# GpSimd adds two rows that nobody reads after each of 128 indirect transfers, in a three-block model on one core

## Chip, core and metric

The kernel runs on one core of a Trainium2 chip. The core has five engines that work in order, each on its own instruction stream, and wait for each other by semaphores: TensorE (PE), VectorE (DVE), ScalarE (ACT), GpSimd (POOL) and SyncE (SP), which here only issues DMA transfers. The metric is the device time of one execution in microseconds (us); lower is better.

## What is computed

The input x is (8, 512, 128). The model is four residual blocks, each behind a layer norm: a delta-rule attention of 16 heads, a mixture of experts, a linear attention of 16 heads, and the same mixture of experts again.

```
x = x + delta_rule_attention(layernorm(x))
x = x + moe(layernorm(x))
x = x + linear_attention(layernorm(x))
x = x + moe(layernorm(x))

def moe(x):                       # 8 experts, 2 per token
    probs = softmax(x @ Wg)
    topw, topi = top_k(probs, 2)  # weights renormalised to a sum of 1
    h = relu(x @ W1[e])           # 128 -> 256
    y = h @ W2[e]                 # 256 -> 128
    return sum over the two experts of topw * y
```

## The kernel before

**Chunks and routes.** The sequence is cut into 8 chunks of 64 steps; a chunk holds 8 x 64 = 512 tokens, as J = 4 tiles of 128 rows. Each of the two mixtures of experts meets each chunk once. These 16 passes are called routes: 0 to 7 are the first mixture, 8 to 15 the second.

**Dense and sparse.** Routes 0 to 5 and 15 are dense: all eight experts are computed for all tokens. Routes 6 to 14 are sparse, in five groups: (6), (7, 8), (9, 10), (11, 12), (13, 14). For a sparse route GpSimd scatters the 512 normalised tokens to DRAM (`s_xs`), each to the places of its two experts: `scatter(r)`, 2 x 4 indirect transfers of 128 rows of 512 B. SP then loads a group's tokens back in tiles of 128 rows of one expert each (`tile_load`, L624, with the weights at L627), two tiles to a pair, 56 pairs in all. TensorE turns a pair (`tile_turn`, L2092), multiplies with W1 (`tile_up`, L2101) and W2 (`tile_down`, L2122); ScalarE copies between them (L1340, L1347, L1354); SP stores the result to `s_ys` (L635). When all tiles of a group are stored, GpSimd collects each token's two rows with `gather(r)`, again 8 indirect transfers, and VectorE adds them with their weights in `combine(r)` (L3118).

**Phases.** Up to about 425 us on the profile's clock the delta rule and the dense routes run, with much work on VectorE. After that TensorE works through the linear attention of 8 chunks and the 56 pairs of tiles, interleaved by hand. The dense route 15 comes last: matmuls at L1814 to L1816 and L2150, ScalarE's relu at L1175, VectorE's mixes at L2743, in eight steps. VectorE has the combines 10 to 14 between the steps of that route: combine 10 ahead of its ranking, combine 12 ahead of the first mix, combine 14 ahead of the last.

**What sets the order.** Every engine's order is written out, one line per step. No scheduler changes it. GpSimd's list after the delta phase is `lin_keep(0)`, `scatter(6)`, `lin_keep(1)`, `scatter(7)`, `scatter(8)`, `lin_keep(2)`, `lin_keep(3)`, `gather(6)`, and so on to `gather(14)`. `lin_keep(c)` (L943) is a sum of 128x512 elements that frees the buffer into which SP loads the next chunk (L536), and whose result VectorE needs in the residual (L3009). `scatter(r)` waits until VectorE has the places of the rows (`row_at`, L3043). `gather(r)` waits until the group's tiles are stored. In SP's list, `tile_load` of a group's first pair waits for all scatters of the group, and everything behind it in the list waits with it. The zero rows that pad the tiles are stored at L597.

The tile `y_odd` is used in the dense routes of the delta phase only. `bo_rows` holds a bias and is never written after its load. `bc(x, 1, J)` repeats a tile J times along a new axis, and `tt` is GpSimd's operation on two tiles.

Of the kernel before, what the change touches and what calls it, by code (L numbers as in the profile page):

```python
# [17 lines left out]

# [1 line left out]

# [6 lines left out]
ALU = mybir.AluOpType  # L29
# [11 lines left out]
J = NT // 128  # L41
# [7 lines left out]
GROUPS = ((6,), (7, 8), (9, 10), (11, 12), (13, 14))  # L49
# [24 lines left out]
def bc(ap, axis, n):  # L74

    ap = ap.unsqueeze(axis)
    shape = list(ap.shape)
    shape[axis] = n
    return ap.to_broadcast(shape)


def build(nc, d, out):
    with ExitStack() as ctx:
        def sb(name, shape, dtype=F32):
            return ctx.enter_context(nc.sbuf_tensor(name, shape, dtype))

        def sem(name):
            return ctx.enter_context(nc.semaphore(name))
# [16 lines left out]
        bo_rows = sb("bo_rows", [128, D])  # L105
# [82 lines left out]
        y_odd = sb("y_odd", [128, J, D])  # L188
# [45 lines left out]
        def slot(r):  # L234
# [16 lines left out]
                 ("pad_at", len(GROUPS) * E), ("tiles", 2 * E), ("first", MOST_TILES), ("expert", MOST_TILES),  # L251
                 ("offset", MOST_TILES), ("counts", E), ("shift", E)]
        low_at = {name: sum(size for _, size in sizes[:k]) for k, (name, _) in enumerate(sizes)}
        low = {name: oq_mem[:, low_at[name]:low_at[name] + size] for name, size in sizes}
        sel_shift = low["sel_shift"].rearrange("p (c e) -> p c e", e=E)
# [100 lines left out]
        tabled, padded, combined = sem("tabled"), sem("padded"), sem("combined")  # L356
        mid_stored, out_stored = sem("mid_stored"), sem("out_stored")
        scattered = [sem(f"scattered_{k}") for k in range(2)]
        gathered = [sem(f"gathered_{k}") for k in range(2)]
        tile_loaded = [sem(f"tile_loaded_{k}") for k in range(BUFFERS)]  # L360
        tile_stored = [sem(f"tile_stored_{k}") for k in range(len(ys))]
# [47 lines left out]
        def _(sp):  # L409
# [180 lines left out]
            def pads(g):  # L590

                sp.wait_ge(tabled, TABLE_OPS * g + 17)
                _, starts_at = nc.values_load_multi_w_load_instructions(
                    pad_at[0:1, g], engines=[mybir.EngineType.SP], min_val=0, max_val=E * ROOM[g] - TILE,
                    skip_runtime_bounds_check_because=ROWS_WHY)
                for e in range(E):
                    sp.dma_start(s_xs[g][bass.ds(starts_at[e], TILE)], zeros[:]).then_inc(padded, 16)  # L597

            def tile_load(p):

                g = sum(2 * p >= first for first in FIRST_TILE[1:])
                k = 2 * p - FIRST_TILE[g]
                sp.wait_ge(tabled, TABLE_OPS * g + 17)
                if k == 0:
                    for par in range(2):
                        mine = [r for r in GROUPS[g] if r % 2 == par]
                        if mine:
                            sp.wait_ge(scattered[par], 16 * 2 * J * (same_parity(mine[-1]) + 1))
                    sp.wait_ge(padded, 16 * E * (g + 1))
                _, at = nc.values_load_multi_w_load_instructions(  # L610
                    tile_table[0:1, g, k:k + 2, 0], engines=[mybir.EngineType.SP], min_val=0, max_val=E * ROOM[g] - TILE,
                    skip_runtime_bounds_check_because=ROWS_WHY)
                _, e = nc.values_load_multi_w_load_instructions(
                    tile_table[0:1, g, k:k + 2, 1], engines=[mybir.EngineType.SP], min_val=0, max_val=E - 1,
                    skip_runtime_bounds_check_because=EXPERT_WHY)
                if p >= BUFFERS:
                    sp.wait_ge(tile_z, p - BUFFERS + 1)
                elif p == 2:
                    sp.wait_ge(y_part, E * N1)
                elif p == 4:  # L620
                    sp.wait_ge(added, EV * N1)
                for h in range(2):
                    b = 2 * (p % BUFFERS) + h
                    sp.dma_start(xs[b], s_xs[g][bass.ds(at[h], TILE)]).then_inc(tile_loaded[p % BUFFERS], 16)  # L624
                for h in range(2):
                    b = 2 * (p % BUFFERS) + h
                    sp.dma_start(w1_tile[b], d["w1"][:, bass.ds(e[h], 1)].rearrange("p o f -> p (o f)")  # L627
                                 ).then_inc(tile_loaded[p % BUFFERS], 16)
# [159 lines left out]
        def _(pool):  # L788
# [14 lines left out]
            tt = nc.gpsimd.tensor_tensor  # L803
# [134 lines left out]
            def lin_keep(c):  # L938

                pool.wait_ge(xb_loaded, 16 * (c + 1))  # L940
                if c:
                    pool.wait_ge(x3_ready, c)
                tt(x_keep[:], x_b[:], bc(bo_rows[:], 1, J), ALU.add).then_inc(kept, 1)  # L943

            def scatter(r):

                k, g = SPARSE.index(r), GROUP_OF[r]
                pool.wait_ge(rows_ready, k + 1)
                pool.wait_ge(xf_ready, J * (r + 1))
                pool.wait_ge(o_part, NG * GROUP_OPS * NCH)  # L950
                for s in range(2):
                    for j in range(J):
                        nc.gpsimd.indirect_dma_start(  # L953
                            s_xs[g], bass.IndirectOffsetOnAxis(ap=row_at[:, k, s, j:j + 1], axis=0),
                            xf_at[r % 2][:, j], None).then_inc(scattered[r % 2], 16)

            def gather(r):

                k, g = SPARSE.index(r), GROUP_OF[r]
                last = FIRST_TILE[g + 1] // 2 - 1  # L960
                for b in range(len(ys)):
                    pool.wait_ge(tile_stored[b], 16 * len([p for p in range(last + 1) if p % len(ys) == b]))
                pool.wait_ge(tabled, TABLE_OPS * (g + 1))
                if k >= 2:
                    pool.wait_ge(combined, 2 * (k - 1))
                for s in range(2):
                    for j in range(J):
                        nc.gpsimd.indirect_dma_start(  # L968
                            gathered_at[k % 2][:, s, j], None, s_ys[g],
                            bass.IndirectOffsetOnAxis(ap=back_at[:, k, s, j:j + 1], axis=0)).then_inc(gathered[k % 2], 16)  # L970

            lin_keep(0)
            scatter(6)
            lin_keep(1)
            scatter(7)
            scatter(8)
            lin_keep(2)
            lin_keep(3)
            gather(6)
            scatter(9)  # L980
            scatter(10)
            lin_keep(4)
            scatter(11)
            gather(7)
            lin_keep(5)
            scatter(12)
            gather(8)
            lin_keep(6)
            scatter(13)
# [2383 lines left out]
```

## Time and profile before

| | us |
|---|---|
| time, median of 3 runs | 790.13 (786.14 to 790.35) |
| span of the profiled execution | 951.4 |
| PE busy | 722.5 (76%) |
| DVE busy | 620.4 (65%) |
| ACT busy | 482.5 (51%) |
| POOL busy | 479.8 (50%) |

The span is the time from the first to the last instruction of the one execution that was profiled. Of that execution no other time is known: what lies around its span isn't given. It is 161 us longer than the median of the runs that were timed without a profile, and the reader has to keep both clocks apart: instants and durations come from the profiled execution, while the time that counts is that of the others.

In a timeline row, the first number is the start, the second the duration, both in us; then engine, line, operation, the tile written and the tiles read, and in square brackets the idle time of the engine just before, with what ended it ("issue" where the profile shows nothing that was waited for, "remote" where it can't name what was). DMA_INDIRECT on POOL is the time in which GpSimd writes the descriptors of one indirect transfer; when its data move is not in that row.

### The profile page before, as it was taken

How to read it: one execution, taken by the hardware profiler on the slowest of the kernel's cores; microseconds unless marked ns; L12 is line 12 of the kernel's file. 1: busy time of each engine (PE TensorE's matmuls, PEld its weight loads, DVE VectorE, ACT ScalarE, POOL GpSimd, SP SyncE). 2: the span in 40 equal slices, each digit the busy share in tenths (PEclk: the TensorE clock that was granted, in tenths of full speed). 3: DMA queues.
4: the chain of work that ended last, by engine and by line, in shares of the span. 5: the costliest groups of instructions: out<-in, count | busy, mean ns of one | idle time of the engine just before them, and what ended most of it. 6: DMA issues, size and time to landing. Idle time of an engine off the chain costs nothing.

```text
span 951.4 us, 17059 instructions
## 1 busy us (share of the span) xinstructions
PE 722.5 (76%) x5202; PEld 588.9 (62%) x5202; DVE 620.4 (65%) x1684; ACT 482.5 (51%) x1270; POOL 479.8 (50%) x550
## 2 busy tenths in 40 slices
PE   5634649888889877878979975798887988199375
PEld 4322428767677756665867865685655868188364
DVE  4789999999999999995754753464434626033224
ACT  4965476979796846474540613243241704054221
POOL 2149896989898989477042033303341122702351
PEclk9865668999999989899875995798777959589697
DMA  5330403040403030103333222234122414335321
GB/s 181 81 81 0 103 11 104 12 114 12 113 11 102 11 103 12 56 1 94 91 97 92 90 68 84 62 89 129 45 87 84 121 45 139 98 101 156 114 73 45
DMA packets 106766, 73.99 MB, mean 78 GB/s; under 512 B 44992, under 2 KB 94656, under 8 KB 106432
## 3 DMA queue, kind: packets, MB, share of 16 engines
q1 hardware_dynamic: 102080, 63.58, 22.8%
q0 software_dynamic: 4608, 9.45, 3.3%
q8 instruction: 39, 0.64, 0.3%
q14 instruction: 39, 0.32, 0.1%
HBM read 45.47 MB, written 27.53 MB: 77 GB/s over the span
## 4 chain that ended last, share of the span: by engine, by line
PE 39%; DVE 27%; issue 13%; another core or an unknown queue 8%; ACT 6%; DMA 3%; POOL 2%; SPq 1%; DVEq 0%; POOLq 0%; ACTq 0%
PE bank L2036 7%; DVE u L2578 6%; PE bank L2122 5%; PE bank L2101 5%; PE bank L2002 5%; DVE hist_mem L2583 4%; DVE hist_mem L2587 4%; DVE prod_mem L2571 3%; PE bank L2092 2%; PE bank L2052 2%; DVE x L2719 2%; PE bank L2040 1%; DMA s_beta<-beta_T 1%; PE bank L1745 1%
## 5 line engine op out<-in xcount | busy, mean ns | idle before, releaser
L1836 PE MATMUL bank<-w,hid 128*128 128x128 f32 x768 | 105.8, 296 | 32.9 <-DVE y_even L2719 17.9
L1836 PEld LDWEIGHTS bank<-w,hid 128*128 128x128 f32 x768 | 99.8, 209 | 44.5 <-issue 13.3
L885 POOL TENSOR_TENSOR oq_mem<-hist_mem,q_t 128x384 f32<-128x384 f32 (+1 forms) x96 | 101.3, 1089 | 0.0
L2578 DVE TENSOR_REDUCE u<-prod_mem 128x32 f32<-128x288 f32 x128 | 86.8, 678 | 3.4
L1175 ACT ACTIVATE hid<-bank 128x512 f32<-128x512 f32 x112 | 62.7, 594 | 50.2 <-PE bank L1816 35.2
L2122 PE MATMUL bank<-w,wv 128*128 x448 | 70.9, 308 | 21.1 <-issue 16.9
L2036 PEld LDWEIGHTS bank<-v_bd,hist_mem 128*64 128x64 f32 x1024 | 74.0, 167 | 17.3 <-issue 17.0
L2036 PE MATMUL bank<-v_bd,hist_mem 128*64 128x18 f32 x1024 | 77.1, 233 | 5.2 <-issue 5.2
L953 POOL DMA_INDIRECT s_xs<-xf,row_at x40 | 39.5, 988 | 81.8 <-DVE row_at L3043 38.1
L2122 PEld LDWEIGHTS bank<-w,wv 128*128 128x128 f32 x448 | 63.8, 218 | 26.3 <-issue 26.1
L1347 ACT ACTIVATE wv<-bank 128x512 f32<-128x512 f32 x56 | 33.7, 602 | 83.7 <-remote 48.6
L968 POOL DMA_INDIRECT qkv<-s_ys,back_at x32 | 31.1, 972 | 86.3 <-DMA s_ys<-q_p 39.2
L943 POOL TENSOR_TENSOR x_in<-x_b,bo_rows 128x512 f32<-128x512 f32 x8 | 10.2, 1270 | 127.4 <-DVE qk L3009 28.5
L2002 PE MATMUL bank<-prod_mem,phi_k 64*64 64x256 f32 x512 | 58.1, 435 | 16.5 <-issue 15.5
L1814 PE MATMUL bank<-xT_h,w_h 128*128 128x512 f32 x112 | 52.8, 471 | 17.3 <-ACT hid L1175 17.1
L1745 PE MATMUL bank<-xnT_h,wtap_h 128*128 128x512 f32 x104 | 49.6, 477 | 20.0 <-DVE qkv L2543 10.4
L2587 DVE TENSOR_REDUCE hist_mem<-hist_mem 128x64 f32<-128x320 f32 x128 | 62.3, 487 | 3.4
L2988 DVE TENSOR_SCALAR den<-bank 128x16 f32<-128x16 f32 x32 | 5.5, 173 | 83.3 <-remote 48.2
L2979 DVE TENSOR_TENSOR hist_mem<-bank,causal 128x1024 f32<-128x1024 f32 x32 | 39.1, 1222 | 26.9 <-PE bank L2002 20.6
L2571 DVE TENSOR_TENSOR prod_mem<-hist_mem,bank 128x256 f32<-128x256 f32 x128 | 53.6, 419 | 4.3 <-ACT bank L1078 0.8
L2583 DVE TENSOR_TENSOR hist_mem<-u,bank 128x256 f32<-128x256 f32 x128 | 53.9, 421 | 3.5
L1307 ACT ACTIVATE prod_mem<-prod_mem,head_mask 128x256 f32<-128x256 f32 x128 | 52.8, 504 | 0.0
(303 smaller groups left out, 1948.6 us busy)
## 6 DMA issues: line engine op xcount, KB each, us to landing
hid<-in_w SPq DMA_DIRECT2D x72, 128.0 KB
s_qkv<-qkv SPq DMA_DIRECT2D x24, 256.0 KB, 3.4
pin<-s_xs SPq DMA_DIRECT2D x76, 64.0 KB
pin<-s_qkv SPq DMA_DIRECT2D x16, 256.0 KB, 2.6
kk<-in_w SPq DMA_DIRECT2D x30, 128.0 KB
s_ys<-q_p SPq DMA_DIRECT2D x28, 128.0 KB
s_ys<-q_t SPq DMA_DIRECT2D x28, 128.0 KB
s_xs<-zeros SPq DMA_DIRECT2D x40, 64.0 KB
```

Source lines behind the costliest of these rows:

```text
L885: tt(oq[:, :, j, :, 0:HD], s_at, bc(turned[:, n, j], 2, HD), ALU.mult).then_inc(o_part, 1)
L1175: nc.scalar.activation(hid[:, e % 2, f], bank[:, ZB + f, :], ACT.Relu).then_inc(hid_ready, 1)
L1307: last = nc.scalar.activation(q_bd[:, h, part], phi_q[:, part], ACT.Copy, scale=head_mask[:, h:h + 1])
L1745: last = nc.tensor.matmul(out_bank, wt[:, k], x[:, :, times], start=(p == 0), stop=(p == len(passes) - 1))
L1836: last = nc.tensor.matmul(bank[:, y_bank(e, wide), tokens], hid[:, e % 2, f, tokens], w2[:, e, f], start=(f == 0), stop=(f == FC - 1))
L2002: last = nc.tensor.matmul(bank[64 * par:64 * par + 64, QB + r, 256 * p:256 * p + 256], phi_k[h, b, 0], q_bd[h, par::2, CH * b:CH * b + CH] ...
L2036: last = nc.tensor.matmul(o[:, 2 * HV * n:2 * HV * n + 2 * HV], att[:, j % 2, r, p, i4], v_bd[:, b, n].rearrange("p r e -> p (r e)"), star ...
L2122: last = nc.tensor.matmul(bank[:, XB, D * h:D * (h + 1)], hid_tile[p % 2][:, at:at + TILE], w2[:, bass.ds(experts[p][h], 1), f].rearrange( ...
L2571: tt(prod[:, n, :, 0:HD], bc(hist[:, n, :, :, BS], 3, BS), bc(nw[2 * n // NB][:, :, t], 1, HD), ALU.mult).then_inc(step, 1)
L2578: red(u[:, n], prod[:, n].rearrange("p m e j -> p m j e"), AX_X, ALU.add).then_inc(step, 1)
L2583: tt(hist[:, n, :, :, 0:BS], bc(u[:, n], 2, HD), bc(k_now[2 * n // NB][:, :, t], 1, HD), ALU.mult).then_inc(step, 1)
L2587: red(hist[:, n + 1, :, :, BS], hist[:, n], AX_X, ALU.add).then_inc(step, 1)
```

## The change

GpSimd gets a helper `pause()`. It adds `bo_rows` to itself over 128x512 elements and writes the sum to `y_odd`, which nobody reads any more. It counts a semaphore of its own, `paused`, and each pause waits for the one before, since both write the same tile. `scatter` calls it after each of its 8 transfers, in all nine sparse routes, `gather` in all but the routes 13 and 14 of the last group. That makes 72 + 56 = 128 pauses. Nothing else changes on any engine.

```diff
+        paused = sem("paused")
...
+            pauses = itertools.count()
+
+            def pause():
+
+                done = next(pauses)
+                if done:
+                    pool.wait_ge(paused, done)
+                tt(y_odd[:], bc(bo_rows[:], 1, J), bc(bo_rows[:], 1, J), ALU.add).then_inc(paused, 1)
+
             def scatter(r):
...
                         nc.gpsimd.indirect_dma_start(
                             s_xs[g], bass.IndirectOffsetOnAxis(ap=row_at[:, k, s, j:j + 1], axis=0),
                             xf_at[r % 2][:, j], None).then_inc(scattered[r % 2], 16)
+                        pause()
...
                         nc.gpsimd.indirect_dma_start(
                             gathered_at[k % 2][:, s, j], None, s_ys[g],
                             bass.IndirectOffsetOnAxis(ap=back_at[:, k, s, j:j + 1], axis=0)).then_inc(gathered[k % 2], 16)
+                        if r not in GROUPS[-1]:
+                            pause()
```

GpSimd's instructions from scatter 13 to the end, before the change: two scatters, gather 9, `lin_keep(7)`, and the gathers 10 to 14, eight transfers each in a row.

```order
L953 DMA s_xs<-squares,row_at 9216x128 x8
L953 DMA s_xs<-xf,row_at 9216x128 x8
L968 DMA qkv<-s_ys,back_at 128x128 x8
L943 TENSOR_TENSOR x_in<-x_b,bo_rows 128x512
L968 DMA sig<-s_ys,back_at 128x128 x8
L968 DMA qkv<-s_ys,back_at 128x128 x8
```

After the change, the end of gather 9, `lin_keep(7)` (now L945) and the start of gather 10 on the same engine; L954 is the pause:

```order
L954 TENSOR_TENSOR y_odd<-bo_rows 128x512
L980 DMA qkv<-s_ys,back_at 128x128
L954 TENSOR_TENSOR y_odd<-bo_rows 128x512
L945 TENSOR_TENSOR x_in<-x_b,bo_rows 128x512
L980 DMA sig<-s_ys,back_at 128x128
L954 TENSOR_TENSOR y_odd<-bo_rows 128x512
```

The transfers keep their order, and one sum stands behind each. The end of GpSimd's list after the change, from the last two transfers of gather 12 on:

```order
L980 DMA sig<-s_ys,back_at 128x128
L954 TENSOR_TENSOR y_odd<-bo_rows 128x512
L980 DMA sig<-s_ys,back_at 128x128
L954 TENSOR_TENSOR y_odd<-bo_rows 128x512
L980 DMA qkv<-s_ys,back_at 128x128 x8
L980 DMA sig<-s_ys,back_at 128x128 x8
```

The last two gathers stand as before. On the other engines nothing has moved.

## Rows read from the trace of the kernel before

**Rows 1.** Windows: stretch, its us, busy us of each engine, granted clock, DMA share, GB/s.
```profile
0.00:425.00 425.00, 309.30 (x1574) 244.09 (x1575) 384.34 (x856) 299.90 (x822) 321.73 (x386) 0.88 0.22 62
425.00:951.40 526.40, 413.24 (x3630) 344.78 (x3628) 236.08 (x829) 182.64 (x448) 158.06 (x165) 0.80 0.30 90
```

**Rows 2.** Timeline of POOL: a sum between two transfers, and gather 11's last transfer.
```profile
818.91 0.94 POOL L968 DMA_INDIRECT qkv<-s_ys,back_at  x1 [0.30 <-issue]
820.16 0.94 POOL L968 DMA_INDIRECT qkv<-s_ys,back_at  x1 [0.30 <-issue]
821.13 1.27 POOL L943 TENSOR_TENSOR x_in<-x_b,bo_rows 128x512 f32<-128x512 f32 x1
822.56 0.96 POOL L968 DMA_INDIRECT sig<-s_ys,back_at  x1 [0.16 <-issue]
...
881.56 0.94 POOL L968 DMA_INDIRECT qkv<-s_ys,back_at  x1 [0.30 <-issue]
```

**Rows 3.** Timeline of PE in the last stretch: matmuls behind idle time.
```profile
812.70 2.07 PE L2122 MATMUL bank<-w,wv 128*128 x8 [6.51 <-issue]
825.44 0.69 PE L2092 MATMUL bank<-ident,y_even 128*128 128x128 f32 x2 [10.67 <-issue]
833.89 2.07 PE L2122 MATMUL bank<-w,wv 128*128 x8 [6.05 <-issue]
...
881.69 1.56 PE L2122 MATMUL bank<-w,wv 128*128 x8 [3.72 <-issue]
895.91 0.69 PE L2092 MATMUL bank<-ident,y_even 128*128 128x128 f32 x2 [12.65 <-ACT wv L1347]
...
932.55 0.79 PE L1814 MATMUL bank<-xT_h,w_h 128*128 128x512 f32 x1 [10.70 <-ACT hid L1175]
```

**Rows 4.** Timeline of ACT: the relu behind the last row of transfers.
```profile
931.90 0.60 ACT L1175 ACTIVATE hid<-bank 128x512 f32<-128x512 f32 x1 [12.89 <-remote]
```

**Rows 5.** Timeline of SP's queue: stores of tiles.
```profile
708.76 14.06 SPq L635 DMA_DIRECT2D s_ys<-q_t  x2
```

**Rows 6.** POOL's waits: for what, us in total, times, longest.
```profile
POOL s_xs L953 <- DVE row_at L3043: 67.2, 6, 17.8
POOL s_xs L953 <- DMA s_ys<-q_p: 33.1, 1, 33.1
```

**Rows 7.** Timeline: last transfers of scatters 6 and 8, first tile loads of their groups.
```profile
450.90 0.96 POOL L953 DMA_INDIRECT s_xs<-xf,row_at  x1 [0.30 <-issue]
454.65 0.90 SPq L624 DMA_DIRECT2D pin<-s_xs  x2
...
507.58 0.96 POOL L953 DMA_INDIRECT s_xs<-xf,row_at  x1 [0.30 <-issue]
514.47 0.90 SPq L624 DMA_DIRECT2D pin<-s_xs  x2
```

**Rows 8.** Timeline of PE: the first turns of tiles of groups 1 and 2.
```profile
466.29 0.44 PE L2092 MATMUL bank<-ident,pin 128*128 128x128 f32 x2
...
533.40 0.38 PE L2092 MATMUL bank<-ident,pin 128*128 128x128 f32 x2
```

**Rows 9.** DVE: rows of route 14, combines 9 and 11, first and last mix.
```profile
800.23 0.17 DVE L3043 CAST row_at<-hist_mem 128x8 int32<-128x8 f32 x1
L3118 DVE SCALAR_TENSOR_TENSOR rqk<-qkv,gate_of,rqk x8: 342/346/352, 858.1 to 860.0; 128x128 f32<-128x128 f32 x8
L3118 DVE SCALAR_TENSOR_TENSOR u<-qkv,gate_of,u x8: 347/348/352, 884.3 to 886.2; 128x128 f32<-128x128 f32 x8
884.26 2.31 DVE L3118 SCALAR_TENSOR_TENSOR u<-qkv,gate_of,u 128x128 f32<-128x128 f32 x8 [2.79 <-DMA qkv<-s_ys,back_at]
912.39 1.13 DVE L2743 SCALAR_TENSOR_TENSOR x<-bank,gate_now,on 128x128 f32<-128x128 f32 x4 [6.16 <-PE bank L2150]
948.05 1.12 DVE L2743 SCALAR_TENSOR_TENSOR x<-bank,gate_now,x 128x128 f32<-128x128 f32 x4
```

More of the change, by code:

```diff
@@ L21 @@
+import itertools
 from contextlib import ExitStack
```

## The prediction

> **What bounds the kernel now.** I read the windows by stage first [rows 1]. Up to 425 us the program is in the delta phase: VectorE is busy for 384.34 of 425 us and no indirect transfer exists there. From 425 us on it is in the sparse phase: TensorE is busy for 413.24 of 526.40 us, at a granted clock of 0.80 on the mean, VectorE for 236.08 and GpSimd for only 158.06. So GpSimd, the only engine that the change touches, is idle for 70% of that phase in the profile.
>
> The second thing to see is that the profile and the timed runs do not agree. The span is 951.4 us, the runs take 790.13 us: 161 us exist only in the profiled execution. The table of waits and the timelines show where. While GpSimd issues a row of indirect transfers, other engines wait for things that are long done: TensorE stands idle before its matmuls for 6.51, 10.67 and 6.05 us between 805 and 834 us, for 3.72 and 12.65 us between 878 and 896 us, and for 10.70 us before 932.55 us [rows 3]; ScalarE takes up at 931.90 us, after 12.89 us of idle time, a bank that TensorE had filled by 920 us [rows 4]. Two stores that SP queues at 708.76 us span 14.06 us together [rows 5]. Each such gap opens 3 to 7 us after the first transfer of a row and closes within 3 us of the last. At first sight the change is made for this: a pause after every transfer would leave room.
>
> Are these gaps in the timed runs? A sum says hardly. The delta phase can't be shorter than VectorE's work, 384.3 us, so the sparse phase takes at most 790.1 - 384.3 = 405.8 us there, at least 120.6 us less than profiled. If the delta phase takes its full 425 us, the sparse phase has 365.1 us. TensorE's work in it is 413.24 x 0.80 = 331 us at full clock, and 376 us at 0.88, the clock of the delta phase [rows 1]. So the timed sparse phase is TensorE back to back with between nothing (365.1 is under 376) and 30 us (405.8 - 376) left for all gaps together. I take the gaps to be mostly the profiler's. In the timed runs the same work is packed about a quarter closer, and GpSimd has less slack than the profile shows.
>
> A rule speaks against this change. The Trainium skill, DMA: Bandwidth & Descriptors, section "SWDGE vs HWDGE vs iDMA", says that transfers of the GpSimd path and those of SP go to different queues of the same DMA engines, which take turns between them, and that SP's never touch GpSimd's descriptor rings. By that rule a row of indirect transfers can't hold SP's for 14 us, and pauses relieve nothing. The profiled trace speaks against it with the 14.06 us above; my reckoning of the timed runs speaks for it.
>
> **The change part by part.** *The pauses.* 72 transfers in nine scatters and 56 in the gathers of routes 6 to 12 get one sum of 128x512 behind each: 128 sums. Only the 16 transfers of the last two gathers follow each other as before. What one costs is in the trace, because the same sum stands once between two transfers: transfer at 820.16 us, sum at 821.13, next transfer at 822.56, thus 2.40 us, against 1.25 us from transfer to transfer without it [rows 2]. So 1.15 us each, where the sum has two tiles as inputs and in the pauses one tile twice. Its wait is for the sum before it, done long ago: nothing. A route of eight transfers takes 19.2 us in place of 10.0, and GpSimd gets 128 x 1.15 = 147 us more work: 158 becomes 305 us, in a phase that lasts 365 to 406 us. That is no longer slack that can be taken for granted, since GpSimd works in order and each scatter waits for its route and each gather for its group's tiles.
>
> *Queued behind the pauses.* SP's loads of a group's first tiles wait for its last scatter, SP's loads of a chunk and VectorE's residual wait for the sum at L943, and VectorE's combines wait for the gathers. Both SP and VectorE work in order too.
>
> *First group.* Scatter 6 ends at 451.86 us [rows 7]; with seven pauses its last transfer leaves 8.1 us later. SP issues the first tile load at 454.65 us and TensorE turns that tile at 466.29 us [rows 7, 8]. Load and landing follow the scatter by about 5 us, so 451.9 + 8.1 + 5 = 465 us: just in time on the profile's clock, and about 2 us late on one where the small gaps of TensorE before 453 us are gone. I book +2 us. The next groups: scatters 7 and 8 end 17 us later, and so the second group's first load could go out at about 530 us in place of 514.47, and TensorE first needs it at 533.40 us [rows 7, 8]; up to +3 us, where I take 0. In the middle GpSimd's waits for rows of routes come to 67.2 us in six cases and 33.1 us in one [rows 6], against 18.4 us that the scatter and the gather of one route get longer: hidden, but with most of the slack gone.
>
> *The last stretch* carries the sum. Route 14, the last sparse one, has its rows ready at 800.4 us (cast at 800.23 [rows 9]) and the span ends 151 us later. From there GpSimd has to do: scatter 14 and gathers 9 to 12, 40 transfers at 2.40 us = 96.0 us; the sum at L943, 1.4 us; then gathers 13 and 14. VectorE's order puts combine 12 ahead of all eight mixes of the last dense route. Combine 12 can start 0.3 + 96.0 + 1.4 + 1.8 us after the rows are ready (0.3 us from them to the first transfer, an "issue" gap as in [rows 2]; 1.8 us is what the data of gather 11 took to land: its last transfer ended at 882.50 us, combine 11 started at 884.26 [rows 2, 9]) and takes 2.3 us: 101.8 us. The mixes run from 912.39 to 949.17 us, 36.8 us, of which 10.7 us is the gap named above: 26.1 us; the last store ends 2.2 us after them. Together 130.1 us. What does the stretch take now in a timed run? 151.1 less the six gaps, 50.3 us, is 100.8 us; by the share of the phase, 151.1 / 526.4 of 365.1 or 405.8 us, it is 105 to 117 us. So the end comes between 13 (130.1 - 117) and 29 us later (130.1 - 101). On the profile's own clock it fits into 151 us and costs nothing. The unmeasured part is the timed stretch, not the pause; I take +19, nearer to the long stretch, because a low clock follows gaps and some of that is probably in the timed runs as well.
>
> *Gains.* At most the 30 us of gaps that fit into the timed sparse phase, at least nothing. I take 5 us of gain. Sum: 790.1 + 2 + 19 - 5 = **806 us**.
>
> *The sum on the shared port.* VectorE's operations with two SBUF inputs take the same time beside transfers as away from them: combine 11 at 0.348 us each, combine 9 at 0.346 us [rows 9]. No row has such an operation beside a GpSimd sum, and VectorE is busy for 45% of this phase, so a hold of one sum, 1.27 us, would mostly fall into idle time: 0, and at worst 2 us per route. The Trainium skill, SBUF — State Buffer, section "SBUF: two separate sides", says that such an operation and a GpSimd operation that reads SBUF shut each other out for a whole instruction. That is in the tail of the range, not in the sum.
>
> **The rivals.** *Faster: the gaps are in the timed runs too.* For it: the profile shows them in every stretch with rows of transfers, and three engines wait, as with something that they share. Against it: the 161 us. With 30 us of gaps in the timed phase of 405.8 us, the last stretch is then 117 us or more, pauses that halve the density clear most of the 30 us, and the late end costs 13 or less: 790 - 27 + 10 = 773 us. It decides from about 20 us of timed gaps on.
>
> *No change: GpSimd's slack covers all.* If the last stretch takes 125 us or more in the timed runs (a uniform shrink, 790 / 951 of 151), 130.1 - 125 is 5, less a few us of gaps: 790 us, 786 to 794.
>
> *The pause doesn't space the transfers.* The busy time of an indirect transfer on GpSimd is the writing of its descriptors. If the data leave later and in their own rhythm, the pauses cost as above and relieve nothing: 808 to 821 us. It has the forecast's sign.
>
> **How the numbers follow.** Forecast, GpSimd becomes what the end waits for: 0.56, 806 us, own range 795 to 826. Faster by freed gaps: 0.28, 773 us. No change: 0.14. Held by the port with little else: 0.02. The range for 8 in 10 takes in most of the faster rival and the late end of the last stretch: 772 to 826 us. A measurement of this kernel tells about 0.5%, 4 us, from no change. Faster by more than that: 0.28, within: 0.14, slower: 0.58.
>
> **What would show it.** In the changed profile GpSimd's transfers should stand 2.40 us apart, and GpSimd should be busy about 160 us longer. The profile's own span may well shrink while the timed runs get slower, since the profiled gaps should be smaller where transfers are spaced: I expect less than half of the 50.3 us of the last stretch to remain, but for the 10.7 us ahead of 932 us, where nothing changes. If the forecast holds, VectorE waits ahead of combines 10 to 12 for the gathers, where it now waits only once, 2.8 us, and gather 13 follows gather 12 without idle time. It is wrong if the timed sparse phase has real gaps, which a time under 786 us would show, or if the last stretch is longer in timed runs than I reckon, which a time near 790 us would.

## Result, and the profile after

The changed kernel takes 874.37 us (873.43 to 874.80), the kernel before in the same comparison 790.24 us: a ratio of 1.109, interval 1.105 to 1.112. It is 84 us slower. The forecast was 806 us; the direction was right, the size was not, and the time lies outside the range.

Line numbers have moved: L943 is L945 now, L3043 is L3057, L3118 is L3132, L2092 is L2106 (L2107 in one experiment); the pause is L954. The windows of the changed kernel, cut where route 14's rows are ready (columns as in [rows 1]):

```profile
425.00:754.00 329.00, 288.12 (x2829) 243.03 (x2830) 246.59 (x665) 137.80 (x349) 198.99 (x196) 0.85 0.34 99
754.00:872.60 118.60, 92.26 (x804) 82.82 (x802) 74.92 (x167) 43.95 (x99) 98.80 (x97) 0.90 0.43 128
```

The delta phase is as before: VectorE is busy for 383.6 of its 425 us, against 383.9 in the run below. To tell where 84 us arise, these windows need a profile of the kernel before that goes with 790 us. [rows 1] does not, as the first experiment shows; its own windows, from a run of 790.0 us with a span of 788.2 us:

```profile
425.00:683.50 258.50, 253.04 (x2830) 215.44 (x2831) 186.96 (x667) 137.11 (x349) 104.17 (x108) 0.99 0.44 125
683.50:788.20 104.70, 91.46 (x803) 83.11 (x801) 48.37 (x165) 43.80 (x99) 55.94 (x57) 0.93 0.51 146
```

So 70.5 us arise ahead of route 14 (329.0 against 258.5) and 13.9 us behind it (118.6 against 104.7). Ahead of it TensorE was busy for all but 5.5 us. With the pauses it does the same 2,830 matmuls in 288 us in place of 253, at a granted clock of 0.85 in place of 0.99 (of its two levels, 2.4 GHz nearly all of the time before), and stands idle for 40.9 us. Of the 70.5 us, half is thus added idle time and half is the same work at a lower clock.

The timeline of POOL, where [rows 2] were read, and the start of gather 13:

```profile
442.24 1.17 POOL L964 DMA_INDIRECT s_xs<-xf,row_at  x1 [4.42 <-DVE row_at L3057]
443.45 1.05 POOL L954 TENSOR_TENSOR y_odd<-bo_rows 128x512 f32<-128x512 f32 x1
444.66 0.99 POOL L964 DMA_INDIRECT s_xs<-xf,row_at  x1 [0.17 <-issue]
...
844.13 1.05 POOL L954 TENSOR_TENSOR y_odd<-bo_rows 128x512 f32<-128x512 f32 x1
845.34 0.96 POOL L980 DMA_INDIRECT qkv<-s_ys,back_at  x1 [0.16 <-issue]
```

Transfers stand 2.2 us apart, and gather 13 follows gather 12 at once. VectorE's groups show something else, by line (mean ns of one before the second bar):

```profile
L2543 DVE TENSOR_SCALAR xn<-x_b,mv,rstd 128x128 f32<-128x128 f32 x28 | 19.0, 739 | 0.5 <-ACT rstd L1070 0.5
L3072 DVE TENSOR_TENSOR gate_of<-hist_mem,rsum 128x8 f32<-128x8 f32 x9 | 10.0, 1109 | 0.3
L3132 DVE SCALAR_TENSOR_TENSOR qk<-sig,gate_of,qk 128x128 f32<-128x128 f32 x8 | 5.8, 785 | 1.4 <-DMA sig<-s_ys,back_at 1.4
```

The same three take 341, 167 and 348 ns in the kernel before. These operations read and write SBUF only, and they take longer while GpSimd's sums run; VectorE is busy 85 us longer from 425 us on. That is as much as the loss, and TensorE's waits name VectorE:

```profile
PE bank L2016 <- DVE hist_mem L2993: 19.8, 6, 6.5
PE bank L2066 <- DVE hist_mem L3012: 9.1, 3, 8.6
PE bank L1808 <- DVE squares L2543: 5.6, 1, 5.6
```

It looks settled: VectorE is held by the sums ("the port" below), which the prediction had priced at nothing. The experiments say otherwise.

### The profile page after: what moved, and what is told of

Read it like the earlier page. It is cut to its first block, busy times and chain, and to the rows that moved or that the text cites. A ratio compares the mean times of both kernels' runs of the same rounds, so it can differ in the third digit from the quotient of the medians.

```text
span 872.6 us, 17187 instructions
## 1 busy us (share of the span) xinstructions
PE 691.7 (79%) x5202; PEld 571.5 (65%) x5202; DVE 705.1 (81%) x1684; ACT 481.4 (55%) x1270; POOL 618.7 (71%) x678
## 4 chain that ended last, share of the span: by engine, by line
DVE 43%; PE 25%; issue 12%; POOL 11%; DMA 5%; ACT 3%; SPq 1%; DVEq 0%; POOLq 0%; ACTq 0%
DVE u L2592 7%; DVE hist_mem L2597 5%; POOL y_odd L954 5%; DVE hist_mem L2601 4%; PE bank L2050 4%; DVE prod_mem L2585 4%; POOL qkv L980 3%; PE bank L2016 3%; PE bank L2136 2%; PE bank L2115 2%; DVE x L2733 2%; PE bank L2066 2%; PE bank L2164 1%; PE bank L1759 1%; DVE o_p L2623 1%
## 5 line engine op out<-in xcount | busy, mean ns | idle before, releaser
L954 POOL TENSOR_TENSOR y_odd<-bo_rows 128x512 f32<-128x512 f32 x128 | 134.2, 1049 | 3.1
L2050 PEld LDWEIGHTS bank<-v_bd,hist_mem 128*64 128x64 f32 x1024 | 69.6, 159 | 16.6 <-issue 11.4
L2050 PE MATMUL bank<-v_bd,hist_mem 128*64 128x18 f32 x1024 | 72.4, 228 | 5.3 <-DVE hist_mem L2993 2.7
L2136 PE MATMUL bank<-w,wv 128*128 x448 | 66.7, 296 | 1.6 <-ACT q_t L1368 0.7
L2136 PEld LDWEIGHTS bank<-w,wv 128*128 128x128 f32 x448 | 60.1, 208 | 6.5 <-issue 6.3
L2016 PE MATMUL bank<-prod_mem,phi_k 64*64 64x256 f32 x512 | 42.2, 454 | 21.8 <-DVE hist_mem L2993 19.8
L964 POOL DMA_INDIRECT s_xs<-squares,row_at x32 | 31.7, 992 | 34.6 <-DVE row_at L3057 29.8
L945 POOL TENSOR_TENSOR x_in<-x_b,bo_rows 128x512 f32<-128x512 f32 x8 | 10.2, 1272 | 63.9 <-DVE qk L3023 28.6
L1829 PE MATMUL bank<-xT_l,w_h 128*128 128x512 f32 x112 | 46.7, 417 | 0.0
```

The lines of the kernel that those rows point to most:

```text
L954: tt(y_odd[:], bc(bo_rows[:], 1, J), bc(bo_rows[:], 1, J), ALU.add).then_inc(paused, 1)
L964: nc.gpsimd.indirect_dma_start(s_xs[g], bass.IndirectOffsetOnAxis(ap=row_at[:, k, s, j:j + 1], axis=0), xf_at[r % 2][:, j], None).then_inc ...
L2016: last = nc.tensor.matmul(bank[64 * par:64 * par + 64, QB + r, 256 * p:256 * p + 256], phi_k[h, b, 0], q_bd[h, par::2, CH * b:CH * b + CH] ...
L2050: last = nc.tensor.matmul(o[:, 2 * HV * n:2 * HV * n + 2 * HV], att[:, j % 2, r, p, i4], v_bd[:, b, n].rearrange("p r e -> p (r e)"), star ...
L2136: last = nc.tensor.matmul(bank[:, XB, D * h:D * (h + 1)], hid_tile[p % 2][:, at:at + TILE], w2[:, bass.ds(experts[p][h], 1), f].rearrange( ...
```

## Experiments

### Two levels of the kernel before

The kernel before was run in every comparison (all kernels of one on the same chip), and has two times: 790 to 792 us in some, 955 to 957 us in others, never one between. One chip showed both, in two comparisons, so it isn't the chip alone; what it is stays open. I call them the low and the high level. Everything is compared within its own comparison.

**The kernel before and after, again.** No edit. Low level.

> The kernel before itself, profiled once more, to see which of two things the first profile was. The runs so far have it at 790 us in one series and at 955 us in another, each steady within 1.5%. Theory C (place): the time depends on the chip, and a profile shows the time of its own chip: the span here is within 3 us of the time here, 790 or 955 us. Theory D (profiler): the profile itself adds the 161 us: the span is 951 us whatever the time.

> The changed kernel beside the kernel before on one chip. If spacing prevents the gaps and nothing else differs between chips, it takes 870 to 880 us here too, whether the kernel before takes 790 us (then it is slower by 84 us) or 955 us (then it is faster by about 80).

Measured: 789.24 us with a profiled span of 788.2, and 875.04 with 870.8 (ratio 1.104, 1.095 to 1.113). For this kernel the profile adds nothing to the time. So the first profile (span 951.4) must have been taken at the high level, and the timed runs at the low one.

**A sum of 8 columns.** High level.

```diff
-                tt(y_odd[:], bc(bo_rows[:], 1, J), bc(bo_rows[:], 1, J), ALU.add).then_inc(paused, 1)
+                tt(y_odd[:, 0, 0:8], bo_rows[:, 0:8], bo_rows[:, 0:8], ALU.add).then_inc(paused, 1)
```

> The pause shrinks from 512 columns to 8: it stays at its 128 places, with its wait, but takes about 0.1 to 0.2 us in place of 1.05. Theory A (port: a sum on GpSimd shuts out VectorE's operations that need the shared port, 85 us of longer VectorE operations) and theory B (queue: GpSimd's 134 us of sums delay what stands behind them) both expect the timed run back near the kernel before, 788 to 805 us. They say nothing about the span of the profile. If the gaps of the old profile come from rows of transfers without any instruction between them, the span falls from 951 to about the timed time; if they come from the density of the transfers, it stays over 900.

**Two memsets, which read nothing.** High level.

```diff
-                done = next(pauses)
-                if done:
-                    pool.wait_ge(paused, done)
-                tt(y_odd[:], bc(bo_rows[:], 1, J), bc(bo_rows[:], 1, J), ALU.add).then_inc(paused, 1)
+                for _ in range(2):
+                    done = next(pauses)
+                    if done:
+                        pool.wait_ge(paused, done)
+                    nc.gpsimd.memset(y_odd[:], 0.0).then_inc(paused, 1)
```

> The pause becomes two clears of y_odd of 128x512, which write and read nothing. The rows of the trace have 1.06 us for a clear of 1152 columns, so two of 512 take about 1.0 to 1.1 us with the wait between them: GpSimd is as busy as with the sums. Theory B (queue) expects no change from the changed kernel: 860 to 880 us. Theory A (port, and only an operation that reads SBUF takes part) expects most of the 84 us back: 795 to 830 us, and VectorE's busy time after 425 us falls from 321 us to under 260.

**The sums behind the row.** High level; eight sums behind each route's eight transfers.

```diff
                             xf_at[r % 2][:, j], None).then_inc(scattered[r % 2], 16)
-                        pause()
+                for _ in range(2 * J):
+                    pause()
...
-                        if r not in GROUPS[-1]:
-                            pause()
+                if r not in GROUPS[-1]:
+                    for _ in range(2 * J):
+                        pause()
```

> The eight pauses of a route come after its eight transfers, not between them: the same work on GpSimd, and each route's data are out 8 us earlier. If the loss is the work on GpSimd (theory A or B), 850 to 875 us; the data leave earlier, so somewhat faster than the change. If it is the spacing as such, near 790 us. In the profile the transfers stand 1.25 us apart again: if density makes the profiler's gaps, the span is well over the timed time again.

Measured, against 955.24: 934.42 (ratio 0.976, 0.971 to 0.982), 875.28 (0.915, 0.910 to 0.919) and 953.96 (0.997, 0.993 to 1.001). At the high level the gaps of [rows 3] are in the timed runs too, and long enough pauses between the transfers remove most of them; the same sums behind the row remove nothing. With two memsets per pause the gain is 80 us. The changed kernel itself was never run at that level; its pause is as long, so a gain of about that size is to be expected there, but isn't shown. TensorE's waits in the run with the sums behind the row, from 425 us on, end mostly with nothing that the profile shows: 21.6 us in 33 small pieces at L2052, 9.7 us in two at L1830, and more.

With the two memsets VectorE is as quick as before (239.7 us busy from 425 us on, where [rows 1] have 236.1), and yet the time is the 875 us that the changed kernel takes at the low level. That was the first sign against the port.

### Scatters, gathers, last stretch

**Pauses in the 72 transfers of the scatters only** (low level), then **in the 56 of the gathers only** (low level): one of the two added `pause()` calls left out.

> Pauses only in the 72 transfers of the scatters; gathers as before. Where the kernel before takes 955 us: the gaps that start in scatters go and those in gathers stay, 900 to 935 us. Where it takes 790: 72 of 128 pauses, and not the ones that the combines at the end wait for, 795 to 830 us.

> Pauses only in the 56 transfers of the gathers 6 to 12. Where the kernel before takes 955 us: 905 to 940 us. Where it takes 790: the gathers 9 to 12 run into the end, 815 to 850 us, more than with the scatters although there are fewer.

Measured: 850.67 (1.070, 1.062 to 1.078) and 820.32 (1.034, 1.026 to 1.042): +59.5 and +29.2 against the 791.17 of the comparison, together 88.7 where both at once cost 83.9. They add up, nearly. Both expectations had the gathers dearer than the scatters; it is the other way round. This split can't tell the port from GpSimd's rows: VectorE's busy time from 425 us on grows by 59.1 and 28.4 us in the two runs, almost exactly as the losses do.

**Pauses from route 14's rows on only**, in scatter 14 and the gathers of routes 9 to 12, 40 transfers.

```diff
-                        pause()
+                        if r == 14:
+                            pause()
...
-                        if r not in GROUPS[-1]:
+                        if r in (9, 10, 11, 12):
                             pause()
```

> Sums only in scatter 14 and the gathers of routes 9 to 12. Where the kernel before takes about 790 us: 802 to 804 us by the traces of the two kernels (104.7 us for the stretch without, 116.8 to 118.6 with sums); the prediction's step said +19, 809 us. Where the kernel before takes 955 us: 930 us as measured.

Measured at the low level: 802.60 against 790.19 (1.015, 1.006 to 1.025), +12.4 us. At the high level twice (expected 802 to 804, or 932 there): 932.03 against 956.28 and 930.93 against 956.78, a gain of 24 to 26 us from 40 pauses. One edit, opposite signs at the two levels.

> Sums only in scatter 14 and in the gathers of routes 9 to 12, the 40 transfers from route 14's rows on (88 of 128 pauses left out). The prediction's step for the last stretch said +13 to +29 us. The traces of the kernel before and of the changed one on undisturbed chips give 104.7 and 116.8 to 118.6 us for it: so +12 to +14 us, 802 to 804 us where the kernel before takes 790. If the last stretch's loss is in truth made earlier and only passed on, 790 to 796 us.

### Held VectorE, or GpSimd's own rows?

**Two memsets per pause, again**, the edit shown above.

> Every pause is two memsets of the same 128x512 tile: GpSimd is busy for as long as with the sum (about 1.07 us per pause by the earlier run), but reads nothing. Theory P (the sum's reads shut VectorE out, VectorE gets late, TensorE waits for it and runs at a lower clock): the middle loss of 59 to 70 us is gone and only GpSimd's longer chain in the last stretch is left, so where the kernel before takes about 790 us this takes 790 to 808 us, VectorE is busy for about 236 us from 425 us on, and TensorE's busy time before route 14's rows falls from 287 us back towards 253. Rival Q (GpSimd's longer rows send the data later, tile loads and combines are late): as the change, 860 to 880 us, with TensorE waiting for loads of tiles. If the kernel before takes about 955 us in this comparison, the run can't tell the two apart (875 by both).

> The two memsets per pause once more, in the hope of a comparison in which the kernel before takes about 790 us. There, theory P (the sum's reads shut VectorE out, VectorE gets late, TensorE waits for it and runs at a lower clock): 790 to 808 us, VectorE busy for about 236 us from 425 us on, TensorE's busy time before route 14's rows back from 287 us towards 253. Rival Q (GpSimd's longer rows make tile loads and combines late): 860 to 880 us.

The first fell into the high level: 874.38 against 956.28, a repeat. The second met the low level: 863.21 us (857.03 to 874.67) against 791.89, ratio 1.091 (1.082 to 1.099). The port was expected to give 790 to 808, GpSimd's own rows 860 to 880. VectorE is hardly held here, 240.9 us busy from 425 us on against 235.3, and 71 of 84 us of the loss are still there. `gate_of` takes its 167 ns again. Only the normalisations still stretch, 496 ns in place of 348 (L2544 here; 514 in the high-level repeat):

```profile
L2544 DVE TENSOR_SCALAR xn<-x_b,mv,rstd 128x128 f32<-128x128 f32 x28 | 9.4, 496 | 0.0
```

The profiled run was the longest of its four, 874.67 us, 11.5 us above their median; what follows of its trace overstates the loss by about that much. Its windows from 425 us to route 14's rows and from there on:

```profile
425.00:753.20 328.20, 273.70 (x2831) 232.91 (x2832) 191.80 (x670) 137.75 (x349) 198.75 (x285) 0.88 0.36 100
753.20:872.90 119.70, 92.62 (x803) 83.78 (x801) 49.05 (x164) 43.68 (x99) 97.37 (x137) 0.90 0.44 123
```

The stretches are as long as in the changed kernel, 328 and 120 us, but TensorE's waits ahead of the turns of tiles (L2107) now name SP's loads, of which the weights (`in_w`) land last:

```profile
PE bank L2107 <- DMA hid<-in_w: 29.2, 2, 17.1
PE bank L2017 <- DVE hist_mem L2994: 9.9, 3, 7.7
```

How the two causes hide each other can be seen in the first group. SP's first load of a tile behind scatter 6, and TensorE's turn of it; in the kernel before at the low level:

```profile
455.66 0.37 SPq L624 DMA_DIRECT2D pin<-s_xs  x1
...
459.93 0.66 PE L2092 MATMUL bank<-ident,pin 128*128 128x128 f32 x2 [1.01 <-DMA kk<-in_w]
```

with the two memsets:

```profile
462.02 0.90 SPq L626 DMA_DIRECT2D pin<-s_xs  x2
...
466.30 0.66 PE L2107 MATMUL bank<-ident,pin 128*128 128x128 f32 x2 [6.47 <-DMA kk<-in_w]
```

and in the changed kernel's second run:

```profile
461.80 0.37 SPq L626 DMA_DIRECT2D pin<-s_xs  x1
...
467.97 0.44 PE L2106 MATMUL bank<-ident,pin 128*128 128x128 f32 x2
```

In all three the turn follows the load by 4.3 to 6.2 us. In the kernel before TensorE is already waiting for it (1.01 us): there is no slack at all. With the memsets the wait for the load is in plain sight, 6.47 us. In the changed kernel VectorE had held TensorE up for 5.79 us (L2993) until 451.94 us, so no wait for the load is left to see. Of two such delays the later one counts, not their sum, and the profile shows only that one. The second group is the same: SP's load stands at 498.44 us before, at 520.17 with the memsets and at 519.89 in the changed kernel; TensorE's turn at 504.99, at 524.39 after 12.10 us of waiting, and at 524.20 after 1.65.

GpSimd's timeline of four kernels at the low level, start of each event in us (K1 to K7 are `lin_keep`):

| | before | changed | two memsets | sums behind the row |
|---|---|---|---|---|
| scatter 6 | 442.3 | 441.3 | 442.6 | 442.3 |
| K1 | 474.5 | 481.5 | 481.4 | 475.3 |
| K2 | 503.0 | 520.4 | 518.8 | 514.8 |
| K3 | 533.9 | 553.9 | 565.3 | 544.6 |
| K4 | 570.2 | 610.9 | 622.0 | 603.0 |
| K5 | 614.6 | 671.3 | 676.9 | 654.3 |
| K6 | 644.2 | 710.4 | 714.7 | 693.2 |
| scatter 14 | 683.8 | 750.8 | 753.3 | 730.0 |
| K7 | 705.0 | 787.0 | 789.3 | 769.1 |
| gather 13 | 761.2 | 841.5 | 846.0 | 827.8 |
| end of span | 788.2 | 870.8 | 872.9 | 856.0 |

The last transfer of a row ends 6.8 us later with pauses (16.83 against 10.02 us after the row's start, scatter 6), and what GpSimd does next starts 7.6 us later (from scatter 7 to scatter 8 17.87 against 10.23 us). Scatter 6 makes K1 7 us later, although GpSimd waits 22 us in between in both kernels; scatters 7 and 8 make K2 another 10.4 later; gather 6, scatters 9 and 10 make K4 another 20.7 later. Eleven rows stand ahead of scatter 14, 84 us of added work, and it comes 67.0 us later. GpSimd's waits tell why its idle time was so little cover. The two longest kinds, before, low level:

```profile
POOL s_xs L953 <- DVE row_at L3043: 34.5, 4, 17.8
POOL x_in L943 <- DVE qk L3009: 29.6, 1, 29.6
```

and in the changed kernel's second run:

```profile
POOL s_xs L964 <- DVE row_at L3057: 43.4, 5, 17.2
POOL x_in L945 <- DVE qk L3023: 32.2, 1, 32.2
```

All its waits for VectorE up to scatter 14 come to 105 us before and 104 after, with 84 us more work between them. Only those for stored tiles shrink, from 22 to 6 us: 16 us of cover in all. With them the sum comes out, 84 - 17 = 67. The reading is this: VectorE's results hang on TensorE, TensorE's order puts a group's tiles ahead of them, and the tiles wait for GpSimd's scatter, so each of these waits starts from GpSimd's own last output. For K1 it is shown, by the table and by the run below; for the later waits it is read from the orders and from waits that keep their length.

**The sums behind the row, at the low level.** It tells which end of a row counts.

> The 128 sums behind each route's eight transfers, for a comparison in which the kernel before takes about 790 us: theory Q (GpSimd's rows are on the path by their length): a group's first tile load is 7 us earlier than in the changed kernel in each of five groups, what GpSimd does behind a row is as late: 840 us, 830 to 855. Rival R (only the departure of the data matters): 795 to 815 us. Rival P (the sums' hold on VectorE): 860 to 880 us. Where the kernel before takes 955 us: 954 to 956 us as measured.

Measured: 862.85 against 790.19 (1.092, 1.078 to 1.105). That is above the 830 to 855 us of the theory, and by the number alone it is what the rival of the held VectorE expected, 860 to 880. The trace speaks against that rival: VectorE is held for 49 us here (284.7 us busy from 425 us on), in the changed kernel for 86, and yet 73 of 84 us of the loss are there. The mechanism of GpSimd's rows shows in the table. K1 is only 0.8 us late: a tile load waits for the last transfer alone. But eight sums in a row make the next work 8.7 us later, not 7.6, because between transfers a sum fills a part of the issue time (scatter 7 starts at 476.69, scatter 8 at 495.66 us: 18.97 in place of 10.23), and they delay what GpSimd does next, K2 by 11.7 us. Scatter 14 is 46 us late in place of 67; the last stretch takes 126.1 us, 21 more than before. I had left the longer row out. At the high level this edit had been run twice more:

> The same 128 sums, but eight in a row behind each route's eight transfers. Where the kernel before takes about 790 us: theory P (reads of the sum shut VectorE out): the same sums hold VectorE about as much, 850 to 880 us, VectorE busy for 270 to 325 us from 425 us on. Rival Q (what costs is that the transfers of a row come apart, so that a group's last data are later by 8 us): a row's transfers leave as early as before, so most of the loss goes: 790 to 815 us.

> The 128 sums, eight in a row behind each route's eight transfers. Where the kernel before takes about 790 us. Theory Q, as it now stands (each row of pauses lengthens GpSimd's own chain, and SP's tile loads and the sums of L945 come later by it, whether VectorE is held or not): what GpSimd does behind a row is as late as in the changed kernel, but a group's first tile load waits only for the eight transfers of its last scatter, 7 us earlier than there, in each of five groups: 875 - 35 = 840 us, 830 to 855. Rival R (only the departure of a row's data matters): 795 to 815 us. Rival P (the sums' hold on VectorE): 860 to 880 us. Where the kernel before takes 955 us: as before, no change.

954.84 against 956.28 and 955.58 against 956.78: no difference, with 134 us more work on GpSimd. There its waits are slack in fact; the gaps, which make all others late, would be a reason, but no run tests that.

### How long a pause

One memset of 128x512 in place of the sum (0.54 us), one of 128x256 (0.33 us), and once more the sum of 8 columns.

```diff
-                tt(y_odd[:], bc(bo_rows[:], 1, J), bc(bo_rows[:], 1, J), ALU.add).then_inc(paused, 1)
+                nc.gpsimd.memset(y_odd[:], 0.0).then_inc(paused, 1)
```

The shorter one writes `y_odd[:, 0:2]`.

> One memset of 128x512 per pause (0.54 us) in place of the sum (1.05 us); it reads nothing. Where the kernel before takes about 790 us: theory Q (GpSimd's chain): half of the loss of the two memsets, 822 to 832 us; if GpSimd had slack that only the second half uses up, 790 to 805 us. Where the kernel before takes about 955 us, it tells how much spacing is wanted there: transfers about 1.75 us apart lie between the tiny sum's 1.5 us (937 us) and the two memsets' 2.2 us (875 us); in proportion 915 us, and 875 to 890 us if there is a threshold below it.

> One memset of 128x256 per pause, about 0.3 us, so transfers some 1.5 us apart; reads nothing. Where the kernel before takes about 955 us: transfers 1.40 us apart (tiny sums) gave 937, 1.74 us apart (one memset of 512 columns) 828. If the holding fades in proportion: about 900 us; if it ends at once somewhere between, and 1.5 is enough: 805 to 815 us; if not: 935 us. Where the kernel before takes about 790 us: theory Q, about 0.25 us per transfer and row by row: 805 to 812 us.

> The sum of a pause has 8 columns (about 0.22 us) in place of 512. Where the kernel before takes about 790 us: P: 128 x 0.22 us of reads instead of 134 us, and no instruction is held for more than 0.2 us: 790 to 798 us. Q: rows of eight transfers get 2 us longer instead of 8, a quarter of the loss: 805 to 815 us.

| pause | transfers apart, median | high level (before: 955 to 957) | low level (before: 790 to 792) |
|---|---|---|---|
| none | 1.27 us | 955.2 | 789.2 |
| 8 columns summed | 1.39 | 934.4, 938.0 | not run |
| memset of 256 columns | 1.46 | not run | 798.9 |
| memset of 512 columns | 1.67 | 827.7 | not run |
| two memsets | 2.2 | 875.3, 874.4 | 863.2 |
| sum of 512 columns | 2.2 | not run | 874.4, 875.0 |

At the high level the gaps lose little at 1.39 us and are nearly gone at 1.67: 827.7 us, ratio 0.860 (0.853 to 0.866), where 875 to 915 had been expected. TensorE's idle time that ends with nothing the profile shows falls from 61.7 us in the first profile to 7.7. Two memsets give 47 us back, with VectorE busy for 240 to 242 us in place of 239. That is a second run against the port: more pause costs, and nothing on VectorE changes. At the low level the short memset costs 8.7 us (ratio 1.012, 1.007 to 1.016), less than the 15 to 22 us expected. An added 0.2 us per transfer, 25 us in all, is mostly covered; an added 0.95 us, 122 us in all, is not.

No version beats the kernel before at the low level, which is the level of the stated time. At the high level one memset does by 129 us.

## Why the prediction was wrong, step by step

**"161 us exist only in the profiled execution", "the gaps are mostly the profiler's".** Wrong as to the cause, nearly right in its consequence. The profile had been taken at the high level; the kernel before has a span of 788.2 us in a profiled run of 790.0. The stage times that the prediction derived for the timed runs came out: sparse phase 365.1 to 405.8 us, measured 363.2 (the time holds 1.8 us that no span shows); last stretch 101 to 117, measured 104.7. In part that is luck, since they were derived as if the profiled execution were a timed run with gaps added.

**First group, +2 us: the first step that failed.** It set scatter 6's later end against TensorE's turn at 466.29 us [rows 7, 8]. That instant came from the high level. The turn stands at 459.93 us at the low level, with TensorE waiting. The prediction had itself worked out that the timed runs were packed a quarter closer, and then read the slack of a step from the stretched trace. Measured: K1 7.0 us later, TensorE's turn 8.0.

**Second group, +3 us at most, 0 taken.** The same error: load at 514.47 and turn at 533.40 us in [rows 7, 8], thus 19 us of slack. At the low level load and turn are 6.5 us apart, and the load comes 21.5 us later. K2 is 17.4 us late.

**The middle, "hidden, but with most of the slack gone", 0: the step that failed by most.** GpSimd's 67.2 and 33.1 us of waits [rows 6] were taken as cover, and set against the 18.4 us of one scatter and one gather. All seven waits together, 100.3 us, would have had to be set against all eleven rows ahead of scatter 14, which by the prediction's own 1.15 us per transfer are 101 us: of the waits that it counted nothing would have been left, even on the profile's clock. And they were waits for work that starts from GpSimd's own rows; this alone makes the middle cost about 50 us (scatter 14 +67.0, K2 +17.4). The three steps, booked at +2, are 67 to 70 us of the loss. The direction was right for 12 to 14 us of it; for the rest the forecast had no reason.

**The last stretch, +19, range 13 to 29.** Held. 118.6 against 104.7 us, 13.9; alone it costs 12.4. The stretch with pauses was put at 130.1 us; the pause is the term that was too dear, 2.19 to 2.22 us from transfer to transfer in place of 2.40 (the sum takes 1.05 us with one tile as both inputs, 1.27 with two [rows 2]), 8 us over 40 transfers. VectorE does wait ahead of its combines, 9.0, 6.6 and 4.9 us; at the low level it did so before the change as well, 3.8, 6.0 and 2.4 us for the same three. This stretch holds the port's effect too: with the 40 pauses alone VectorE is busy 26 us longer, and no run separates the two there.

**Gains, 5 us.** None: TensorE is idle for 5.5 us ahead of route 14 at the low level.

**The shared port, 0.** The size of the hold was misjudged (85 us of VectorE, not 2 us per route), in line with the rule of the Trainium skill, SBUF — State Buffer, section "SBUF: two separate sides", that had been set aside: `gate_of`, which has two SBUF inputs, takes 1109 ns beside the sums and 167 beside memsets. But it decides little: almost without the hold the loss is 71 us, with it 84. The other rule that was weighed, the Trainium skill, DMA: Bandwidth & Descriptors, section "SWDGE vs HWDGE vs iDMA", speaks of a separation of queues; the 14.06 us of [rows 5] remain as evidence against reading it as independence at the high level.

**The rivals.** "Faster: the gaps are in the timed runs too" was given 773 us. It holds at the high level only, where nothing had been timed. "No change: GpSimd's slack covers all" fell on the middle. "The pause doesn't space the transfers" is not borne out at the high level, where pauses between the transfers win 18 to 129 us and the sums behind the row win nothing; at the low level there are no gaps to relieve.

**The signs.** Transfers stand 2.2 us apart, not 2.40. GpSimd is busy 140 us longer (297.8 against 158.1), not 160; the prediction's own sum had said 147. Gather 13 follows gather 12 at once, as expected, and that sign came although the forecast left out most of the loss. The profile's span did shrink while the timed runs got slower, but because the two profiles are of different levels.

What is not shown: what sets the level; how much of TensorE's lower clock is a cause of its own (at the low level it is lower where TensorE's idle time is larger, from 0.97 with 19 us in the kernel before to 0.88 with 68 in the changed one, though not in strict order: with two memsets it is 0.89 with 82); and whether the hold adds its 12 us or the two comparisons differ (the four runs behind 863.2 ranged up to 874.7). The two-memset kernel met the low level in one comparison only.

## What to carry to other kernels

Before a trace is used for slack, see that its span agrees with the time that is to be explained. If not, its durations may serve, but the distance between a result and its first use may not, since that is just what changes. An engine's idle time covers added work only if what ends the wait doesn't itself start from that engine's output: follow the releaser back one round before booking a zero. And when one suspected cause shows large in the profile, take it away before believing it; a second one of nearly the same size may stand behind it.

## What was not expected of the hardware

Rows of GpSimd's indirect transfers 1.27 us apart slow the other engines at one level (955 us) and not at the other (790 us), the same program on the same chip. At the slow one 1.67 us between them is enough (828 us) and 1.39 is not (934). Beside GpSimd's sums, which read SBUF, a VectorE operation of 0.17 us takes 1.1 us on the mean (`gate_of`). GpSimd's memset, which only writes, leaves that one at 0.17 us, but stretches VectorE's normalisations with one tile as input from 0.35 to 0.50 us (L2544); in all VectorE is busy for 240.9 against 235.3 us from 425 us on.
